# Every matmul of the delta stage set to 128 rows and 128 columns, with zero weights in what is added

## The chip, the cores and the metric

The kernel runs on one core of one Trainium2 chip. The metric is the device time of one execution in microseconds (us), and the median of the runs counts.

## The reference, cut to what matters

A state-space block over an image of 48 x 48 places and 256 channels (two images, four channel groups: 8 units `u`) is followed by attention and a mixture-of-experts layer. The change is in the step that prepares the scan of the first layer, the delta stage:

```python
x = x @ in_W                                   # 64 -> 128 channels
x = conv_general_dilated(x, conv_W, ...)       # 3x3, depthwise
x = silu(x + conv_b)
xs = stack([x0, x1, x0 reversed, x1 reversed]) # 4 directions k
dbl = einsum('bkdl,kcd->bkcl', xs, x_proj_W)
dts, Bmat, Cmat = split(dbl, [4, 20], axis=2)
delta = softplus(einsum('bkrl,kdr->bkdl', dts, dt_W) + dt_b)
... scan over l with delta, delta*u, Bmat, Cmat ...
```

## The kernel before, in words

The program runs in stages, each a block of five instruction streams (TensorE, VectorE, ScalarE, GpSimd, SyncE) that meet through semaphores: setup, norm0, delta, scan, merge, norm1, projection, attention, gate, experts. A stage starts when the one before it has ended.

The delta stage (`delta_phase`, L282 on) has these matmuls, all with 128 output columns but one:

- **convolve** (L412): input projection and 3 x 3 convolution in one. An image tile `img` holds the image twice, in rows 0 to 63 and, shifted by one line, in rows 64 to 127. A block of 384 places (`TT`) takes six taps: three with `w_pair` (128 rows, two image lines at a time) alternate with three with `w_one` (64 rows, the third line; it reads only rows 0 to 63 of `img`). A tap has 384 columns of moving data, or 376 at the image's edges. Each tap is float32, and the profile shows it as two weight loads and two matmuls.
- **project** (L428): 384 places of `xs` or its transposed copy `xt` by `w_bc`, 128 rows by 96 columns, float32, again two loads and two matmuls.
- **expand** (L438, L439): pieces of 512 (`PIECE`) by `w_dt` (104 rows) and then by `w_dt_lo` (64 rows), both float32r, one load and one matmul each. The tile `cut` that they read holds in rows 0 to 39 the projected values as float32r, ones in the rest up to row 63, and in rows 64 to 103 what the rounding left (`lo`).

The work is cut into 16 groups `g` (8 units, 2 pairs of directions `p`), nine pieces each. The order on TensorE is written out by hand: first, ahead of the groups, nine blocks of convolve (six of unit 0, three of unit 1), then six projects for group 0; then for each piece `i` of a group an expand, in six of the nine pieces a project for the next group, and in six pieces three taps of a convolve for a unit to come (so three blocks per group, up to group 12; groups 13 to 15 have none, group 15 has no project either). PSUM holds three pieces of `ps_a`, three of `ps_e`, but one `ps_b` and one `ps_c`: a project waits until ScalarE and VectorE have taken the block before, a convolve until VectorE has copied the block out (L511).

ScalarE makes the magnitude (L475), the exponential (L495), copies of the projected blocks (L470, L471), at the end of a group three logarithms of 1536 (L480) and, in every second group, a silu of the next unit (L461); a table load stands between each kind. VectorE has per piece L547, L551, L555, then the addition of the logarithm for the group before (L525, six per group), and takes the blocks (L511, L517, L519). GpSimd multiplies (L575) and transposes (L567); SyncE stores.

The first thing VectorE does in the stage is to clear `img` and write the ones of `cut` (L528 to L533); the semaphore `cleared` then lets SyncE load the first image, which the first convolve waits for. The weights are made in `setup_phase` (L74 on): `w_one` at L172, `w_dt` at L159, `w_dt_lo` at L181.

Of the kernel before, what the change touches and what calls it, by code (L numbers as in the profile page):

```python
# [6 lines left out]
F32 = mybir.dt.float32  # L7
BF16 = mybir.dt.bfloat16
F32R = mybir.dt.float32r
U32 = mybir.dt.uint32  # L10
I32 = mybir.dt.int32
ALU = mybir.AluOpType
# [8 lines left out]
DM = C // BR  # L21
D = 128
K = 4
R, N = 4, 16
# [2 lines left out]
HW_ = WC // 2  # L27
STEPS = K * NCH
PAIRS = 2
STACK = 104  # L30
PIECE = 512
SOFT = (4, 12)
WARM = (1, 3, 6, 8, 10, 13, 15)
# [3 lines left out]
TT = 384  # L37
# [36 lines left out]
def setup_phase(nc, P, w, keep):  # L74

    with ExitStack() as ctx:
        s = Space(nc, ctx, "setup")
        dt_raw = s.sb("dt_raw", [STACK, K, D])
        x_rows = s.sb("x_rows", [R + 2 * N, K, D])
        conv_taps = s.sb("conv_taps", [128, D, 9])  # L80
        in_w2 = s.sb("in_w2", [128, D])
# [5 lines left out]
        loaded, ones_set, ident_set = s.sem("loaded"), s.sem("ones_set"), s.sem("ident_set")  # L87
# [73 lines left out]
        @block.vector  # L161
        def _(dve):
            dve.wait_ge(exp_done, 1)
            dve.wait_ge(pool_set, 4)
            dve.wait_ge(pool_set, 5)
            dve.tensor_scalar(keep["a_neg"][:, :, :], a_exp[:, :, :], -1.0, None, ALU.mult).then_inc(a_done, 1)

            for dx in range(3):
                for half in range(2):
                    p = slice(64 * half, 64 * half + 64)  # L170
                    dve.tensor_tensor(keep["w_pair"][p, dx, :], in_w2[p, :], conv_taps[p, :, 3 * half + dx], ALU.mult)
                dve.tensor_tensor(keep["w_one"][:, dx, :], in_w2[0:64, :], conv_taps[0:64, :, 6 + dx], ALU.mult)  # L172
            dve.tensor_reduce(keep["d_sum"][:, :], ds4[:, :], AX.X, ALU.add)
            dve.wait_ge(bc_ps, 1)
            for p in range(PAIRS):
                for k in range(2):
                    d = p + 2 * k
                    for to, at, n in ((N * k, R, N), (2 * N + R * k, 0, R), (4 * N + N * k, R + N, N)):
                        dve.tensor_copy(keep["w_bc"][:, p, to:to + n], ps_w[:, d, at:at + n])
            dve.wait_ge(dt_cut, 1)  # L180
            dve.tensor_tensor(keep["w_dt_lo"][:, :, :], dt_raw[0:64, :, :], keep["w_dt"][0:64, :, :].bitcast(F32), ALU.subtract)  # L181


def norm_phase(nc, tag, src, dst, keep):
# [96 lines left out]
def delta_phase(nc, P, keep):  # L281
# [4 lines left out]
    with ExitStack() as ctx:  # L286
# [4 lines left out]
        bc = [s.sb(f"bc{i}", [6 * N, L]) for i in range(2)]  # L291
        cut = [s.sb(f"cut{i}", [STACK, L], F32R) for i in range(2)]
        mag = [s.sb(f"mag{i}", [128, PIECE]) for i in range(3)]
        de = [s.sb(f"de{i}", [128, 2 * L]) for i in range(2)]
        du = [s.sb(f"du{i}", [128, 2 * L]) for i in range(2)]
        ps_a = [s.ps(f"ps_a{i}", [128, PIECE]) for i in range(3)]
        ps_e = [s.ps(f"ps_e{i}", [128, PIECE]) for i in range(3)]
        ps_b = s.ps("ps_b", [128, PIECE])
        ps_c = s.ps("ps_c", [128, PIECE])
        cleared, ones_set, xs_ready, xt_ready = s.sem("cleared"), s.sem("ones_set"), s.sem("xs_ready"), s.sem("xt_ready")  # L300
# [4 lines left out]
        a_full, b_full, c_full, c_taken = (s.sem(x) for x in ("a_full", "b_full", "c_full", "c_taken"))  # L305
        even_taken, odd_taken, hi_done, lo_done = (s.sem(x) for x in ("even_taken", "odd_taken", "hi_done", "lo_done"))
# [85 lines left out]
        @block.tensor  # L392
        def _(pe):
            def convolve(unit, t, first, last):
                o = ps_c[:, 0:TT]
                ov = o.rearrange("p (r w) -> p r w", w=W)
                iv = img[unit % 2][:, :].rearrange("p (r w) -> p r w", w=W)
                r0 = t * (TT // W)
                RB = TT // W
                if first == 0:  # L400
                    if t == 0:
                        pe.wait_ge(img_here[unit % 2], 32 * (unit // 2) + 32)
                    pe.wait_ge(c_taken, unit * TPI + t)
                taps = [(dx, one) for dx in (1, 0, 2) for one in range(2)]
                for n in range(first, last):
                    dx, one = taps[n]
                    a, b = max(0, 1 - dx), min(W, W + 1 - dx)
                    if one:
                        lhs, rows, x = keep["w_one"][:, dx, :], slice(r0 + 2, r0 + 2 + RB), iv[0:64]
                    else:  # L410
                        lhs, rows, x = keep["w_pair"][:, dx, :], slice(r0, r0 + RB), iv
                    mm = pe.matmul(ov[:, :, a:b], lhs, x[:, rows, a + dx - 1:b + dx - 1], start=n == 0, stop=n == 5)  # L412
                if last == 6:
                    mm.then_inc(c_full, 1)

            def project(g, b):
                u, p = divmod(g, PAIRS)
                m = TPI * g + b
                if b == 0:
                    if p == 0:  # L420
                        pe.wait_ge(xs_ready, u + 1)
                    else:
                        pe.wait_ge(xt_ready, u + 1)
                if m:
                    pe.wait_ge(lo_done, m)
                    pe.wait_ge(even_taken, (m + 1) // 2)
                x = xs[u % 3] if p == 0 else xt[u % 2]
                pe.matmul(ps_b[0:6 * N, 0:TT], keep["w_bc"][:, p, :], x[:, b * TT:b * TT + TT], start=True, stop=True).then_inc(b_full, 1)  # L428

            def expand(g, i):  # L430
                n = g * IG + i
                pe.wait_ge(hi_done, TPI * g + blocks_for(i))
                pe.wait_ge(lo_done, TPI * g + blocks_for(i))
                if n >= 3:
                    pe.wait_ge(v_done, n - 2)
                for r, at, a, b in spans(i):
                    d = g % PAIRS + 2 * r
                    pe.matmul(ps_a[n % 3][:, a:b], keep["w_dt"][:, d, :], cut[g % 2][:, at:at + b - a], start=True, stop=False)  # L438
                    mm = pe.matmul(ps_a[n % 3][:, a:b], keep["w_dt_lo"][:, d, :], cut[g % 2][0:64, at:at + b - a], start=False, stop=True)  # L439
                mm.then_inc(a_full, 1)  # L440

            for t in range(TPI):
                convolve(0, t, 0, 6)
            for t in range(3):
                convolve(1, t, 0, 6)
            pe.wait_ge(ones_set, 2)
            for b in range(TPI):
                project(0, b)
            for g in range(G):
                for i in range(IG):  # L450
                    expand(g, i)
                    if proj_block(g, i):
                        project(*proj_block(g, i))
                    if conv_block(g, i) and i % 3 < 2:
                        convolve(*conv_block(g, i), 3 * (i % 3), 3 * (i % 3) + 3)
# [48 lines left out]
        def _(dve):  # L504
# [8 lines left out]
            def take_block(g, b):  # L513
                m = TPI * g + b
                dve.wait_ge(hi_done, m + 1)
                if m % 2:
                    dve.tensor_copy(bc[g % 2][:, b * TT:b * TT + TT], ps_b[0:6 * N, 0:TT]).then_inc(odd_taken, 1)  # L517
                at = slice(b * TT, b * TT + TT)
                dve.tensor_tensor(cut[g % 2][64:STACK, at], ps_b[0:40, 0:TT], cut[g % 2][0:40, at].bitcast(F32), ALU.subtract).then_inc(lo_done, 1)  # L519

            def add_log(g, j):
                at = slice(j * WC, j * WC + WC)
# [4 lines left out]
            for k in range(2):  # L527
                dve.memset(img[k][:, :], 0.0)  # L528
            for k in range(2):
                last = dve.memset(cut[k][32:64, :].bitcast(F32), 1.0)  # L530
                last.then_inc(ones_set, 1)
            last = dve.memset(mag[0][:, 0:1], 0.0)
            last.then_inc(cleared, 1)  # L533
            for t in range(TPI):
# [5 lines left out]
            for g in range(G):  # L540
                for i in range(IG):
                    n = g * IG + i
                    at = slice(i * PIECE, i * PIECE + PIECE)
# [1316 lines left out]
def conv_attn_hybrid_kernel(nc, x, w0, w1, out):  # L1860
# [15 lines left out]
    with ExitStack() as ctx:  # L1876
# [4 lines left out]
        }  # L1881
        scan_shapes = {
            "ones_d": [128, 128], "a_neg": [D, K, N],
            "w_bc": [128, PAIRS, 6 * N], "w_pair": [128, 3, D], "w_one": [DM, 3, D],
            "conv_b": [D, 1], "onorm_g": [D, 1], "onorm_b": [D, 1], "out_W": [D, DM], "d_sum": [D, 1],
            "skip": [DM, 1],
        }
        keep = {name: s.sb(name, shape) for name, shape in shapes.items()}
        with nc.cleanup_on_exit(), ExitStack() as mamba:
            m = Space(nc, mamba, "layer0")  # L1890
            keep |= {name: m.sb(name, shape) for name, shape in scan_shapes.items()}
            keep["b_sel"] = m.sb("b_sel", [128, N, 128], F32R)
            keep["w_dt"] = m.sb("w_dt", [STACK, K, D], F32R)
            keep["w_dt_lo"] = m.sb("w_dt_lo", [64, K, D], F32R)
            setup_phase(nc, P, w0, keep)
            norm_phase(nc, "norm0", x.rearrange("b c y x -> b c (y x)"), P["xn"], keep)
            delta_phase(nc, P, keep)
            scan_phase(nc, P, keep)
            merge_phase(nc, P, keep)
# [37 lines left out]
```

## Time and profile before

| | |
|---|---|
| median of three runs | 6650.8 us (6642.84 to 6655.27) |
| the profiled execution | 6642.5 us, its span 6640.5 us |
| TensorE matmuls, share of the span | 84% |
| VectorE, ScalarE, GpSimd | 67%, 57%, 61% |
| granted TensorE clock, mean over the span | 0.874 of full |

The granted clock has two levels, 0.5 (1.2 GHz) and 1.0 (2.4 GHz). In a view by windows, each row gives the window, its length, and for each engine the busy time and the number of instructions, then the granted clock, the mean busy share of the DMA engines and their rate. In a view by groups of instructions, a row gives line, engine, operation, tiles, shapes, count, busy time, mean ns of one, and the idle time of the engine just before them. For a matmul, `104*128` is rows by columns of the weights. In a timeline, a row gives start, length, and what ran; equal neighbours are merged (x2), and the bracket is idle time of the engine before it with what ended it.

### The profile page before, as it was taken

Reading aid. Unit: us, or ns where it says so; the run is one execution under the profiler, and the core shown is the slowest. Engines: PE = TensorE matmul, PEld = TensorE weight load, DVE = VectorE, ACT = ScalarE, POOL = GpSimd, SP = SyncE. Lnnn points to the kernel's source line nnn. Section 1 sums busy time; section 2 is a strip of 40 time slices with the busy share of each in tenths; the row PEclk is TensorE's granted clock in tenths of the full one; section 3 lists DMA queues with packets and bytes.
Section 4 is the critical chain, followed back from the end, with each engine's and each line's share of the span. In section 5 each row is a group of like instructions: output and inputs, shape, how many; then the busy total and the mean of one; then the engine's idle time right before and its main releaser. Section 6 shows DMA issues by size and latency. Waiting matters only on the chain. (4 is left out here: it accounts for less than half of the span.)

```text
span 6640.5 us, 85890 instructions
## 1 busy us (share of the span) xinstructions
PE 5592.6 (84%) x22476; PEld 3598.1 (54%) x22476; DVE 4455.1 (67%) x4543; ACT 3776.0 (57%) x8015; POOL 4033.4 (61%) x2715
## 2 busy tenths in 40 slices
PE   4888876999989899898998999955579999965995
PEld 2233323555555555555555555532359999944773
DVE  2355568999999999999999999967331111144332
ACT  2234356888778778787877878844542222232232
POOL 0022226999999999999999999953014444412441
PEclk7555557999999999999999999987789999975897
DMA  2133336777777777777777777766200000012213
GB/s 78 67 121 135 121 134 230 247 248 248 245 243 245 238 245 248 239 245 243 246 247 244 245 243 249 249 211 215 91 29 0 0 0 0 0 50 87 76 58 107
DMA packets 399683, 1073.52 MB, mean 162 GB/s; under 512 B 51470, under 2 KB 94511, under 8 KB 393600
## 3 DMA queue, kind: packets, MB, share of 16 engines
q1 hardware_dynamic: 387808, 1043.07, 47.7%
q0 software_dynamic: 7584, 20.72, 1.0%
q10 hardware_dynamic: 3840, 4.72, 0.3%
q8 instruction: 160, 2.62, 0.2%
q14 instruction: 291, 2.38, 0.1%
HBM read 883.39 MB, written 184.94 MB: 161 GB/s over the span
## 5 line engine op out<-in xcount | busy, mean ns | idle before, releaser
L910 POOL TENSOR_TENSOR scan_hc<-scan_h,scan_c_rep 128x768 f32<-128x768 f32 x1536 | 2743.8, 1828 | 257.3 <-PE scan_ps_y L741 224.9
L741 PE MATMUL scan_ps_y<-scan_hc,keep_ident 128*128 128x512 f32 (+1 forms) x6144 | 2223.0, 489 | 24.7 <-ACT scan_y L776 21.1
L875 DVE TENSOR_TENSOR_SCAN scan_h<-scan_da,scan_h,scan_ps_p 128x768 f32<-128x768 f32 x896 | 1573.5, 1795 | 0.0
L741 PEld LDWEIGHTS scan_ps_y<-scan_hc,keep_ident 128*128 128x128 f32 x6144 | 1068.8, 191 | 829.4 <-issue 745.7
L832 ACT ACTIVATE scan_da<-scan_dd,layer_a_neg 128x768 f32<-128x768 f32 x1344 | 1209.7, 926 | 189.0 <-DVE scan_h L875 184.1
L793 ACT ACTIVATE scan_warm<-scan_du_t 128x128 f32<-128x128 f32 x4032 | 1243.4, 389 | 3.8 <-PE scan_ps_p L732 3.2
L1252 POOL TENSOR_TENSOR attn_e_lo<-attn_e,attn_e_hi 128x384 fp32r<-128x384 f32 x432 | 437.1, 1012 | 773.5 <-DVE attn_e_hi L1243 773.5
L875 DVE TENSOR_TENSOR_SCAN scan_h<-scan_da,scan_ps_p 128x768 f32<-128x768 f32 x448 | 760.9, 1734 | 2.0 <-ACT scan_da L832 2.0
L854 DVE TENSOR_TENSOR scan_ps_p<-scan_ps_p,scan_dd 128x768 f32<-128x768 f32 x672 | 634.9, 945 | 134.5 <-PE scan_ps_p L724 132.7
L1243 DVE CAST attn_e_hi<-attn_e 128x384 fp32r<-128x384 f32 x432 | 165.4, 383 | 713.3 <-ACT attn_e L1231 713.3
L732 PE MATMUL scan_ps_p<-keep_ident,scan_warm 128*128 128x128 f32 x4032 | 579.9, 280 | 68.6 <-DVE scan_h L875 63.6
L1231 ACT ACTIVATE attn_e<-attn_ps_s 128x384 f32<-128x384 f32 x432 | 212.6, 492 | 692.6 <-PE attn_ps_s L71 692.6
L724 PE MATMUL scan_ps_p<-scan_cut,layer_b_sel 128*128 128x512 f32 x1344 | 434.4, 404 | 159.0 <-DVE scan_h L875 156.9
L732 PEld LDWEIGHTS scan_ps_p<-keep_ident,scan_warm 128*128 128x128 f32 x4032 | 444.7, 142 | 212.3 <-issue 134.7
L724 PEld LDWEIGHTS scan_ps_p<-scan_cut,layer_b_sel 128*128 128x128 f32 x1344 | 219.2, 190 | 341.1 <-DVE scan_h L875 312.5
L904 POOL TENSOR_TENSOR scan_bu<-scan_dd,scan_b_rep 128x768 f32<-128x768 f32 x192 | 350.5, 1826 | 0.0
L575 POOL TENSOR_TENSOR delta_du<-delta_de,delta_xs 128x768 f32<-128x768 f32 x48 | 86.8, 1808 | 415.4 <-DVE delta_de L525 415.4
L475 ACT ACTIVATE delta_mag<-delta_ps_a 128x512 f32<-128x512 f32 x144 | 85.7, 595 | 433.7 <-PE delta_ps_a L439 433.6
L412 PE MATMUL delta_ps_c<-delta_img,layer_w_pair 128*128 128x376 f32 (+1 forms) x288 | 232.3, 910 | 108.0 <-DVE delta_xs L511 75.3
L547 DVE TENSOR_SCALAR delta_du<-delta_ps_e 128x512 f32<-128x512 f32 x144 | 99.0, 688 | 322.9 <-ACT delta_ps_e L495 322.9
L69 PE MATMUL attn_ps_s<-f_hi,f_lo 128*128 x864 | 293.1, 339 | 2.1 <-DVE attn_t_lo L1239 2.1
L69 PE MATMUL attn_ps_o<-attn_e_hi,attn_t_lo 128*128 128x384 f32 x864 | 291.5, 337 | 3.7 <-POOL attn_e_lo L1252 3.7
(282 smaller groups left out, 8190.4 us busy)
## 6 DMA issues: line engine op xcount, KB each, us to landing
scan_c_rep<-bc_dram SPq DMA_DIRECT2D x1536, 384.0 KB, 4.3
scan_dd<-dd_dram SPq DMA_DIRECT2D x96, 768.0 KB, 5.7
scan_b_rep<-bc_dram SPq DMA_DIRECT2D x192, 384.0 KB, 4.9
dd_dram<-delta_de SPq DMA_DIRECT2D x96, 384.0 KB, 2.4
dd_dram<-delta_du SPq DMA_DIRECT2D x96, 384.0 KB, 3.0
y_dram<-scan_y SPq DMA_DIRECT2D x96, 384.0 KB, 4.6
merge_y<-y_dram SPq DMA_DIRECT2D x32, 1152.0 KB, 10.6
delta_img<-xn_dram SPq DMA_DIRECT2D x16, 576.0 KB, 9.8
```

The costliest lines, as they stand in the source:

```text
L69: pe.matmul(out, wl, xh, start=start, stop=False)
L412: mm = pe.matmul(ov[:, :, a:b], lhs, x[:, rows, a + dx - 1:b + dx - 1], start=n == 0, stop=n == 5)
L724: mm = pe.matmul(ps_p[place(t) % PR][:, lo:hi], keep["b_sel"][:, n, :], cut[st % 2][:, lo:hi], start=True, stop=True)
L732: mm = pe.transpose(ps_p[place(t) % PR][:, b * 128:b * 128 + 128], warm[w % WR][:, b, :], keep["ident"][:, :])
L741: mm = pe.matmul(ps_y[:, lo:hi], keep["ident"][:, :], hc[t % HR][:, lo:hi], start=n == 0, stop=n == N - 1)
L793: last = act.activation(warm[w % WR][:, b, :], du_t[st % 2][:, b * 128:b * 128 + 128], ACT.Identity, scale=du_t[st % 2][:, at:at + 1])
L832: act.activation(dst, dd[st % 2][:, 0, :], ACT.Exp, scale=keep["a_neg"][:, k, n:n + 1]).then_inc(ex_done, 1)
L854: dve.tensor_tensor(x, x, dd[st % 2][:, 1, :], ALU.mult).then_inc(mult_done, 1)
L875: dve.tensor_tensor_scan(view(h[n]), view(x), view(y), start, ALU.mult, ALU.add).then_inc(scan_done, 1)
L904: pool.tensor_tensor(bu[f % SR][:, :], dd[st % 2][:, 1, :], b_rep[f % SR][:, :], ALU.mult).then_inc(bu_done, 1)
L910: pool.tensor_tensor(hc[t % HR][:, :], h[t % N][:, :], c_rep[t % CR][:, :], ALU.mult).then_inc(hc_done, 1)
L1252: pool.tensor_tensor(e_lo[j % 4][:, :], e[j % 4][:, :], e_hi[j % 4][:, :].bitcast(F32), ALU.subtract).then_inc(lo_done, 1)
```

## The change

`STACK` goes from 104 to 128, so `w_dt` and `cut` get 128 rows; `w_dt_lo` and `w_one` get 128 rows with zeros in rows 64 to 127; `w_bc` gets 128 columns with zeros in the last 32. The matmuls with `w_one` now read all 128 rows of `img`, those with `w_dt_lo` all 128 of `cut`. VectorE clears the new parts.

```diff
-STACK = 104
+STACK = 128
...
             dve.wait_ge(pool_set, 4)
+            dve.memset(keep["w_one"][64:128, :, :], 0.0)
+            dve.memset(keep["w_dt_lo"][64:128, :, :].bitcast(F32), 0.0)
...
-                dve.tensor_tensor(keep["w_one"][:, dx, :], in_w2[0:64, :], conv_taps[0:64, :, 6 + dx], ALU.mult)
+                dve.tensor_tensor(keep["w_one"][0:64, dx, :], in_w2[0:64, :], conv_taps[0:64, :, 6 + dx], ALU.mult)
...
-            dve.tensor_tensor(keep["w_dt_lo"][:, :, :], dt_raw[0:64, :, :], keep["w_dt"][0:64, :, :].bitcast(F32), ALU.subtract)
+            dve.tensor_tensor(keep["w_dt_lo"][0:64, :, :], dt_raw[0:64, :, :], keep["w_dt"][0:64, :, :].bitcast(F32), ALU.subtract)
...
                     if one:
-                        lhs, rows, x = keep["w_one"][:, dx, :], slice(r0 + 2, r0 + 2 + RB), iv[0:64]
+                        lhs, rows = keep["w_one"][:, dx, :], slice(r0 + 2, r0 + 2 + RB)
                     else:
-                        lhs, rows, x = keep["w_pair"][:, dx, :], slice(r0, r0 + RB), iv
-                    mm = pe.matmul(ov[:, :, a:b], lhs, x[:, rows, a + dx - 1:b + dx - 1], start=n == 0, stop=n == 5)
+                        lhs, rows = keep["w_pair"][:, dx, :], slice(r0, r0 + RB)
+                    mm = pe.matmul(ov[:, :, a:b], lhs, iv[:, rows, a + dx - 1:b + dx - 1], start=n == 0, stop=n == 5)
...
-                pe.matmul(ps_b[0:6 * N, 0:TT], keep["w_bc"][:, p, :], x[:, b * TT:b * TT + TT], start=True, stop=True).then_inc(b_full, 1)
+                pe.matmul(ps_b[:, 0:TT], keep["w_bc"][:, p, :], x[:, b * TT:b * TT + TT], start=True, stop=True).then_inc(b_full, 1)
...
-                    mm = pe.matmul(ps_a[n % 3][:, a:b], keep["w_dt_lo"][:, d, :], cut[g % 2][0:64, at:at + b - a], start=False, stop=True)
+                    mm = pe.matmul(ps_a[n % 3][:, a:b], keep["w_dt_lo"][:, d, :], cut[g % 2][:, at:at + b - a], start=False, stop=True)
...
-                dve.tensor_tensor(cut[g % 2][64:STACK, at], ps_b[0:40, 0:TT], cut[g % 2][0:40, at].bitcast(F32), ALU.subtract).then_inc(lo_done, 1)
+                dve.tensor_tensor(cut[g % 2][64:104, at], ps_b[0:40, 0:TT], cut[g % 2][0:40, at].bitcast(F32), ALU.subtract).then_inc(lo_done, 1)
...
             for k in range(2):
-                last = dve.memset(cut[k][32:64, :].bitcast(F32), 1.0)
-                last.then_inc(ones_set, 1)
+                dve.memset(cut[k][64:STACK, :].bitcast(F32), 0.0)
+                dve.memset(cut[k][32:64, :].bitcast(F32), 1.0).then_inc(ones_set, 1)
+            dve.wait_ge(ones_set, 2)
             last = dve.memset(mag[0][:, 0:1], 0.0)
             last.then_inc(cleared, 1)
...
-            "w_bc": [128, PAIRS, 6 * N], "w_pair": [128, 3, D], "w_one": [DM, 3, D],
+            "w_bc": [128, PAIRS, 128], "w_pair": [128, 3, D], "w_one": [128, 3, D],
...
-            keep["w_dt_lo"] = m.sb("w_dt_lo", [64, K, D], F32R)
+            keep["w_dt_lo"] = m.sb("w_dt_lo", [STACK, K, D], F32R)
```

## Rows read from the trace of the kernel before

**Rows 1.** Windows over the delta stage, cut where its parts begin.
```profile
115.40:205.40 90.00, 84.69 (x108) 26.96 (x108) 4.46 (x8) 2.21 (x1) 4.07 (x1) 0.50 0.14 36
205.40:232.70 27.30, 19.15 (x27) 6.00 (x26) 5.53 (x10) 7.12 (x14) 0.00 (x0) 0.50 0.03 12
232.70:279.50 46.80, 41.36 (x58) 14.86 (x58) 22.65 (x37) 13.96 (x27) 0.00 (x0) 0.50 0.05 19
279.50:939.80 660.30, 578.43 (x816) 204.29 (x814) 354.85 (x539) 267.83 (x397) 154.97 (x78) 0.52 0.34 126
939.80:1011.20 71.40, 44.95 (x65) 16.32 (x65) 56.76 (x87) 44.37 (x67) 25.87 (x13) 0.50 0.47 179
```

**Rows 2.** Waits of the stage: who for whom, us in total, times, longest.
```profile
ACT delta_mag L475 <- PE delta_ps_a L439: 433.6, 129, 8.0
DVE delta_du L547 <- ACT delta_ps_e L495: 322.9, 81, 8.3
```

**Rows 3.** Timeline of TensorE: taps of the first and second block.
```profile
116.99 1.65 PE L412 MATMUL delta_ps_c<-delta_img,layer_w_one 64*128 64x384 f32 x2
118.56 1.62 PE L412 MATMUL delta_ps_c<-delta_img,layer_w_pair 128*128 128x376 f32 x2
120.11 1.62 PE L412 MATMUL delta_ps_c<-delta_img,layer_w_one 64*128 64x376 f32 x2
...
125.48 1.65 PE L412 MATMUL delta_ps_c<-delta_img,layer_w_pair 128*128 128x384 f32 x2 [0.65 <-DVE delta_xs L511]
```

**Rows 4.** Timeline of weight loads in the norm stage, 384 columns each.
```profile
66.24 0.33 PEld L230 LDWEIGHTS norm_ps_m<-norm_x,keep_ones_c 128*128 128x128 f32 x1 [0.30 <-issue]
66.88 0.33 PEld L230 LDWEIGHTS norm_ps_m<-norm_x,keep_ones_c 128*128 128x128 f32 x1 [0.31 <-issue]
```

**Rows 5.** Windows: the norm stage's second burst, then the early scan stage.
```profile
65.40:68.60 3.20, 3.16 (x5) 1.83 (x6) 0.20 (x1) 0.00 (x0) 0.00 (x0) 0.50 1.02 347
68.60:82.00 13.40, 13.40 (x43) 7.85 (x42) 5.53 (x6) 8.95 (x12) 0.00 (x0) 1.00 0.12 44
...
1162.00:1330.00 168.00, 152.92 (x655) 93.52 (x656) 163.36 (x115) 136.99 (x300) 157.92 (x90) 1.00 0.75 248
```

**Rows 6.** TensorE in a short stretch at full clock: timeline, then window.
```profile
567.81 0.90 PE L412 MATMUL delta_ps_c<-delta_img,layer_w_pair 128*128 128x376 f32 x2
568.64 0.90 PE L412 MATMUL delta_ps_c<-delta_img,layer_w_one 64*128 64x376 f32 x2
...
567.00:573.80 6.80, 4.95 (x13) 1.85 (x12) 4.81 (x8) 4.42 (x9) 0.00 (x0) 1.00 0.13 54
```

**Rows 7.** Logarithms of ScalarE that end groups 12, 13 and 14.
```profile
939.79 4.23 ACT L480 ACTIVATE delta_du<-delta_du 128x1536 f32<-128x1536 f32 x3
...
977.24 1.49 ACT L480 ACTIVATE delta_du<-delta_du 128x1536 f32<-128x1536 f32 x1
...
1011.15 1.48 ACT L480 ACTIVATE delta_du<-delta_du 128x1536 f32<-128x1536 f32 x1
```

**Rows 8.** VectorE by line, in group 14, then in group 1.
```profile
L547 DVE TENSOR_SCALAR delta_du<-delta_ps_e 128x512 f32<-128x512 f32 x10 | 6.8, 684 | 4.8 <-ACT delta_ps_e L495 4.8
...
L511 DVE COPY delta_xs<-delta_ps_c 128x384 f32<-128x384 f32 x3 | 1.6, 548 | 0.0
```

**Rows 9.** The longest wait of VectorE between groups 12 and 13.
```profile
DVE delta_du L547 <- ACT delta_ps_e L495: 7.4, 1, 7.4
```

**Rows 10.** Timeline of VectorE at the start of the stage, and in setup.
```profile
100.50 2.06 DVE L528 MEMSET delta_img<- 128x2400 f32 x1 [0.45 <-issue]
...
105.48 1.98 DVE L530 MEMSET delta_cut<- 32x2304 f32 x1 [0.43 <-issue]
...
25.89 0.68 DVE L181 TENSOR_TENSOR layer_w_dt_lo<-setup_dt_raw,layer_w_dt 64x512 fp32r<-64x512 f32 x1 [10.53 <-ACT layer_w_dt L159]
```

**Rows 11.** Weight loads of the stage by line and shape.
```profile
L412 PEld LDWEIGHTS delta_ps_c<-delta_img,layer_w_pair 128*128 128x128 f32 x288 | 71.4, 308 | 237.2 <-issue 116.9 <-DVE delta_xs L511 87.0 <-DMA delta_img<-xn_dram 33.3
L428 PEld LDWEIGHTS delta_ps_b<-delta_xs,layer_w_bc 128*96 128x96 f32 x96 | 18.7, 255 | 54.8 <-ACT delta_xs L461 23.8 <-DVE delta_cut L519 17.6 <-issue 13.4
```

## Prediction

> **What bounds the kernel now.** I read the windows first, to find the stage. From 115.4 to 1011.2 us TensorE runs nearly all the time at a granted clock of 0.5, that is 1.2 GHz, and it is busy for 84.69 of 90.00 us in the convolve prologue and for 578.43 of 660.30 us in groups 1 to 12 [rows 1]. VectorE is busy only 354.85 us there. The waits say the same: ScalarE waits 433.6 us for `ps_a`, VectorE 322.9 us for the exponential behind it [rows 2]. So in the groups with a convolve TensorE sets the pace.
>
> Groups 13 and 14 have no convolve, and there the bound changes. Their logarithms start 37.45 and 33.91 us after the one before [rows 7], against 660.3 / 12 = 55.0 us in groups 1 to 12. In group 14 VectorE waits once, 4.8 us, for the logarithms and the table load of ScalarE [rows 8]; in group 13, which follows a silu, 7.4 us [rows 9]. The rest it is busy, so these two are VectorE's own pace.
>
> **What a matmul of another width costs today.** Two things show.
>
> First, gaps. A tap of 384 columns takes 118.56 - 116.99 = 1.57 us, one of 376 takes 1.55 [rows 3]. The norm stage has the same float32 matmul with 128 rows each time: its loads stand 66.88 - 66.24 = 0.64 us apart, 1.28 for two, at the same clock [rows 4, 5]. So a tap loses 0.29 to 0.30 us where rows go from 128 to 64 or back. At full clock a tap takes 568.64 - 567.81 = 0.83 [rows 6] against 1.28 / 2 x 376 / 384 = 0.63, a loss of 0.20. By piece kind (expand, three taps; expand, project, three taps; expand, project) the row count crosses 64 four, six and two times, if 104 counts as full; that is 12 in three pieces, 36 in a group.
>
> Second, the clock. The norm burst rose to 1.0 about 3.2 us after its start, all its matmuls having 128 rows [rows 5]. The convolve prologue, 94% busy with 128 and 64 rows in turn, stays at 0.50 for 90 us [rows 1]. That points to rows as what counts. Whether zero weights count is shown by the scan stage: most of its matmuls use the identity as weights, 127 of 128 entries zero, at a clock of 1.00 [rows 5].
>
> The Trainium skill (TensorE: Matmul & The Clock Gate, Part 1) says that the clock follows how busy TensorE has been and names no rows. By that the prologue should have been granted full clock, which the trace contradicts; what the rule would leave of the change is the second rival below.
>
> **The change part by part.**
>
> Setup: two clears on VectorE of 384 and 512 elements, each below the 0.68 us of the same-size subtraction at L181. VectorE waits 10.5 us ahead of L181 [rows 10] for the `dt` loads, which hides them; uncovered they would cost 1.4. Taken at nothing.
>
> Start of the stage: two more clears of 2304 elements ahead of `cleared`. The one with 32 rows takes 1.98 us after a gap of 0.43 [rows 10]; with 64 rows the trace has none. A clear of 2400 elements on 128 rows takes 2.06, so rows don't lengthen it, and I take 2.41 each; were it to go by rows, double. +4.9 us, all on the path, since the first image load and the first tap wait for it. At most +9.6.
>
> Convolve prologue, 90.0 us now: nine blocks, each six taps, and nine waits of 0.65 for VectorE's copy [rows 3]. With no gaps and at full clock a block is 6 x 0.63 = 3.8 us; the first, partly at half clock, 5.5. Together 5.5 + 8 x 3.8 + 9 x 0.65 = 41.8: -48.2. The silu of unit 0 (2.21 us in the prologue window [rows 1]) still ends before the last of these blocks.
>
> Project prologue, 27.3 us [rows 1]: a chain of TensorE, ScalarE and VectorE for each of six blocks; TensorE idles in every link of it, so I count no clock and only the shorter matmul, about 0.2 each: -1. With full clock -5.
>
> Group 0, 46.8 us [rows 1], of which VectorE is busy 22.65. With a wait like group 14's 4.8 and some 5 us for taps at half clock just after the idle stretch: about 33, -14.
>
> Groups 1 to 12, 660.3 us. TensorE: busy 578.43 / 12 = 48.2 us a group; without 36 gaps of 0.295, 37.6; at full clock 18.8. VectorE: group 14's pace plus three copies of `ps_c`, 1.6 us and their starts [rows 8], so 33.9 + 1.7 = 35.6, and 37.45 + 1.7 = 39.1 after a silu. TensorE at 18.8 lies well below, so VectorE is late next: 6 x 35.6 + 6 x 39.1 = 448. But during VectorE's wait TensorE runs out of buffers, idles and may lose the clock, as it did after 573.8, where it had been busy 4.95 of 6.80 us [rows 6], and the next taps restart at half rate. It is two to three pieces ahead, which covers most of this; I leave 1 us a group. 448 + 12 = 460: -200. Bounds: ScalarE further ahead could hide one or two logarithms, 1.4 us a group less; the upper bound is rival one.
>
> Groups 13 to 15 and the tail are at VectorE's pace already: nothing. GpSimd was busy 25.87 and DMA 0.47 of 71.4 us at that pace [rows 1], so neither takes over. The 32 more columns of `w_bc` lengthen its load from 255 to about 308 ns [rows 11], hidden behind the matmul before once widths are equal, as in the norm stage.
>
> Sum: 4.9 - 48.2 - 1 - 14 - 200 = -258. Against the profiled execution's 6642.5 us that is 6384; the median of the runs stands 8.3 above it, so **6392 us**. This case alone: 6365 to 6420.
>
> **The rivals.**
>
> *One, the clock is lost in every group and costs more.* For: VectorE's pace keeps TensorE busy only half the time, and one short idle took the clock at 573.8. Against: TensorE even at half clock needs 37.6 us a group, about what VectorE needs. If each group loses 3 to 5 us instead of 1, +24 to +48: 6416 to 6440.
>
> *Two, the clock doesn't follow rows and only the gaps go.* Then the prologue loses 54 x 0.295 = 16, groups 1 to 12 lose 12 x 36 x 0.295 = 127, group 0 10, project 1, plus 4.9: -149, 6502. Against: the norm and the prologue differ in rows above all. For: another cause, such as how the taps' rows are read, can't be excluded. This is also the time where zero rows aren't counted for the clock. It is what the Trainium skill's rule (TensorE: Matmul & The Clock Gate, Part 1) would come to, if equal widths remove the gaps.
>
> *Three, neither follows width*: gaps belong to changing weights, the clock to something else. Against: the identity and other weights alternate in the scan stage at full clock. Then only the clears are left, 6656, no change that can be measured.
>
> *Four, slower.* As three, with the gaps before each load kept and the `w_bc` load exposed: 192 loads of 53 ns more, 10.2 us [rows 11], with the clears 15: 6666. It decides from 13.3 us on, which is 0.2%, about what a measurement of this kernel can tell from no change.
>
> **How the numbers follow.** Forecast 0.73, rival one 0.12, two 0.08, three 0.05, four 0.02. Faster by over 0.2%: the first three, 0.93; within 0.2% 0.05; slower 0.02. The range starts below the forecast's own, since logarithms hidden behind VectorE would take 17 more and two executions differ by 10: 6355. It ends at 6450, with rival one inside; rivals two to four and a small part of the forecast, under 0.2 together, are left out.
>
> **What would show it.** Right: clock near 1.0 from about 125 us until the first project, a tap at 0.64 us; 4.9 us from the last old clear to the new start; groups 35 to 41 us apart, with VectorE waiting 3 to 8 us once a group; groups 13 to 15 unchanged. Wrong: clock at 0.5 through the prologue with taps at 1.28 (rival two) or 1.57 (three); inside the groups many waits of VectorE for the exponential (rival one); time gained or lost behind the delta stage.

## The result, and the profile after

The changed kernel runs in 6383.4 us (median of four, 6381.9 to 6389.1) against 6647.2 for the kernel before (four runs, the three shown and one more): ratio 0.960, 95% interval 0.959 to 0.962. Faster by 264 us, 4.0%. The forecast was 6392, with 6365 to 6420 for this case alone and 6355 to 6450 as the whole range.

The windows over the delta stage, cut at the same events as in [rows 1] (first tap, first project, logarithms of groups 0, 12 and 14):

```profile
121.90:167.00 45.10, 38.96 (x110) 20.93 (x110) 5.01 (x9) 2.96 (x3) 4.10 (x1) 0.96 0.28 71
...
214.80:676.50 461.70, 323.49 (x816) 178.59 (x816) 348.74 (x540) 261.45 (x398) 155.61 (x78) 0.83 0.49 180
676.50:746.80 70.30, 38.02 (x64) 16.23 (x64) 56.60 (x86) 44.31 (x66) 25.92 (x13) 0.51 0.48 184
```

The same number of matmuls (816) in groups 1 to 12 takes 461.7 us instead of 660.3, and the granted clock is 0.83 instead of 0.52. VectorE's busy time is unchanged (348.7 against 354.9 us), but it is now 76% of the stretch instead of 54%. Groups 13 and 14 take 70.3 us, as before within 1.1. (The first window here runs 1.7 us past the first project, which starts at 165.4: the prologue itself is 43.4 us.)

The waits of groups 1 to 12 (engine and line, who was waited for, us in total, times, longest), two of the kernel before and then three of the changed one; [rows 2] count the whole stage. VectorE waits far less for the exponential, three times a group instead of six. TensorE waits for VectorE's copy of `ps_c` as often as before, but longer:

```profile
DVE delta_du L547 <- ACT delta_ps_e L495: 276.4, 72, 8.3
PE delta_ps_c L412 <- DVE delta_xs L511: 66.4, 36, 2.7
...
DVE delta_du L550 <- ACT delta_ps_e L497: 102.8, 36, 7.7
PE delta_ps_c L414 <- DVE delta_xs L513: 99.5, 36, 3.0
PE delta_ps_b L430 <- ACT delta_xs L463: 18.8, 6, 3.3
```

The timeline of the first taps answers to [rows 3] and [rows 4]:

```profile
121.91 1.65 PE L414 MATMUL delta_ps_c<-delta_img,layer_w_pair 128*128 128x384 f32 x2 [37.63 <-DMA delta_img<-xn_dram]
123.35 1.48 PE L414 MATMUL delta_ps_c<-delta_img,layer_w_one 128*128 128x384 f32 x2
124.63 1.05 PE L414 MATMUL delta_ps_c<-delta_img,layer_w_pair 128*128 128x376 f32 x2
125.52 0.80 PE L414 MATMUL delta_ps_c<-delta_img,layer_w_one 128*128 128x376 f32 x2
126.15 0.80 PE L414 MATMUL delta_ps_c<-delta_img,layer_w_pair 128*128 128x376 f32 x2
```

The second tap (`w_one`, now 128 rows) starts 1.28 us before the third at half clock, where it took 1.57 before. From 125.1 us on the clock is full, and a tap takes 0.63 us. From there on each tap of the prologue is therefore 2.5 times as fast as it was.

Where the 258 us between the two profiled executions (6642.5 and 6384.8) are:

| part | before, us | after, us | difference |
|---|---|---|---|
| up to the first tap | 115.4 | 121.9 | +6.5 |
| convolve prologue | 90.0 | 43.4 | -46.6 |
| first project to the logarithms of group 0 | 74.1 | 49.5 | -24.6 |
| groups 1 to 12 | 660.3 | 461.7 | -198.6 |
| groups 13 to 15 | 98.5 | 97.2 | -1.3 |
| all that follows | 5604.2 | 5611.1 | +6.9 |

The last row runs from the last logarithms of the delta stage to the end. Of its 6.9 us, 2.6 lie between these logarithms and the scan stage's first instruction (23.8 us before, 26.4 after). From that instruction to the end of the span it is 5578.4 and 5582.8 us; the instructions there are the same, and over the twelve profiles of this study that part varies from 5578 to 5598 us. So I don't lay those 4.4 us to the change, but no run shows that it has no share in them.

### The profile page after: what moved, and what is told of

It is laid out like the page before. It is cut to its first block and busy times, and to the rows that moved or that the text cites. A ratio compares the mean times of both kernels' runs of the same rounds, so it can differ in the third digit from the quotient of the medians.

```text
span 6382.9 us, 85894 instructions
## 1 busy us (share of the span) xinstructions
PE 5254.0 (82%) x22476; PEld 3561.1 (56%) x22476; DVE 4453.9 (70%) x4547; ACT 3769.1 (59%) x8015; POOL 4035.1 (63%) x2715
## 5 line engine op out<-in xcount | busy, mean ns | idle before, releaser
L71 PE MATMUL attn_ps_s<-f_hi 128*128 x864 | 293.8, 340 | 0.0
L70 PE MATMUL attn_ps_s<-f_lo,f_hi 128*128 x864 | 292.6, 339 | 0.0
L71 PE MATMUL attn_ps_o<-attn_e_hi,attn_t_hi 128*128 128x384 f32 x864 | 291.6, 337 | 0.0
L70 PE MATMUL attn_ps_o<-attn_e_lo,attn_t_hi 128*128 128x384 f32 x864 | 290.2, 336 | 0.0
```

Source lines behind the costliest of these rows:

```text
L70: pe.matmul(out, wh, xl, start=False, stop=False)
L71: return pe.matmul(out, wh, xh, start=False, stop=stop)
```

## The experiments

Two causes were in play, which the kernel before mixes: **gaps** where the row count crosses 64, and the **clock**. Of the clock I had claimed that it follows active rows; the rival is that it was kept low by the gaps themselves, since matmuls without gaps are also denser. "Prologue" below is first tap to first project.

### Half of the change at a time

`e1_conv_only` is the kernel before with only the third-line taps widened:

```diff
+            dve.memset(keep["w_one"][64:128, :, :], 0.0)
...
-                        lhs, rows, x = keep["w_one"][:, dx, :], slice(r0 + 2, r0 + 2 + RB), iv[0:64]
+                        lhs, rows, x = keep["w_one"][:, dx, :], slice(r0 + 2, r0 + 2 + RB), iv
```

> Only the convolve's third-line taps (w_one) get 128 rows; expand and project stay as before. Theory (rows carry the clock, each crossing of 64 rows costs a gap of 0.2 to 0.3 us, VectorE's pace is the floor): the convolve prologue is like that of the changed kernel, about 45 us at clock 1.0; in the groups 18 crossings are left instead of 36, TensorE needs about 43 us a group at half clock and 22 at full, so VectorE still sets nearly all of the pace: 6385 to 6410 us. Rival (the 104- and 64-row matmuls hold the clock at 0.5 inside the groups): 48 us a group, about 6490.

`e2_expand_only` is the changed kernel with those taps narrow again:

```diff
-                        lhs, rows = keep["w_one"][:, dx, :], slice(r0 + 2, r0 + 2 + RB)
+                        lhs, rows, x = keep["w_one"][0:64, dx, :], slice(r0 + 2, r0 + 2 + RB), iv[0:64]
```

> Everything widened but the convolve, whose third-line taps keep 64 rows. Theory: the convolve prologue stays at clock 0.5 with taps of 1.55 us, 90 us, 45 more than in the changed kernel; in the groups 18 crossings and mostly half clock, 46 to 50 us a group: 6500 to 6550 us. Rival (it is the expand's rows that hold the clock down in the groups, and the convolve's matter little there): groups near 38.5 us as in the changed kernel, 6430.

Measured: 6411.4 us, ratio 0.963 (0.961 to 0.965), and 6510.0 us, ratio 0.978 (0.976 to 0.979). Their windows, prologue and groups 1 to 12, the first kernel first:

```profile
116.80:160.90 44.10, 38.80 (x108) 21.05 (x109) 4.46 (x8) 2.22 (x1) 4.10 (x1) 0.95 0.29 74
217.30:702.50 485.20, 373.93 (x816) 180.13 (x816) 350.03 (x541) 263.26 (x397) 155.32 (x78) 0.77 0.47 171
```

```profile
123.30:213.30 90.00, 84.70 (x109) 26.96 (x109) 4.46 (x8) 2.22 (x1) 4.07 (x1) 0.50 0.14 36
270.90:803.50 532.60, 405.13 (x816) 175.22 (x816) 352.30 (x541) 261.29 (x397) 155.25 (x78) 0.74 0.42 156
```

The convolve carries most: with it alone the prologue is won and the groups fall to 40.4 us each; 248 of 264 us are there, and the total is 1 us above the range that theory gave it. The other half alone leaves the prologue at 90.0 us and half clock, to the tenth of a microsecond the old one. In its groups I was off: I expected mostly half clock and 46 us or more, and got 0.74 and 44.4. A group's mix of wide taps, expands and projects lifts the clock although every third-line tap stays narrow. So neither half needs the other, and their gains don't add.

### Gaps or rows

`e5_gap_full` gives the changed kernel its gaps back without taking a row away; the small matmul adds zero:

```diff
+                    if n:
+                        pe.matmul(ov[:, 0, 0:8], keep["w_one"][64:128, 0, :], img[unit % 2][64:128, 0:8], start=False, stop=False)
                     mm = pe.matmul(ov[:, :, a:b], lhs, iv[:, rows, a + dx - 1:b + dx - 1], start=n == 0, stop=n == 5)
```

> The changed kernel, with a tiny matmul of 64 rows and 8 columns with zero weights between the taps of the convolve, so that each tap has its gaps back while its rows stay 128. Theory (rows count for the clock): clock 1.0 in the prologue, a tap about 0.9 to 1.0 us, prologue 55 to 60 us. Rival (what kept the clock low before was the gaps, not the rows): clock 0.5 in the prologue, a tap about 1.7 us, prologue 95 to 100 us.

`e9_conv_80` does the opposite. All taps use 80 rows, so nothing crosses 64, and a part of the contraction is left out:

```diff
-                        lhs, rows = keep["w_one"][:, dx, :], slice(r0 + 2, r0 + 2 + RB)
+                        lhs, rows, x = keep["w_one"][0:80, dx, :], slice(r0 + 2, r0 + 2 + RB), iv[0:80]
...
-                        lhs, rows = keep["w_pair"][:, dx, :], slice(r0, r0 + RB)
+                        lhs, rows, x = keep["w_pair"][0:80, dx, :], slice(r0, r0 + RB), iv[0:80]
```

> The changed kernel, but all taps of the convolve use only the first 80 rows (a part of the contraction is left out). No tap crosses 64 rows, so no gaps. Theory (active rows carry the clock): clock 0.5 in the prologue, taps of 1.28 us without gaps, prologue about 75 us. Rival (gaps kept the clock low): clock 1.0, taps 0.64 us, prologue 45 us. If 80 rows had gaps against 128, taps would show 1.55 us.

The prologue of the kernel with gaps in two windows, then two taps of its timeline at full clock, with the small matmul between them:

```profile
121.40:138.00 16.60, 15.95 (x30) 7.22 (x30) 0.56 (x1) 0.00 (x0) 0.00 (x0) 0.51 0.22 47
138.00:193.40 55.40, 50.75 (x171) 25.11 (x171) 3.90 (x7) 2.21 (x1) 4.10 (x1) 1.00 0.16 43
...
151.50 0.91 PE L416 MATMUL delta_ps_c<-delta_img,layer_w_one 128*128 128x384 f32 x2
152.34 0.39 PE L415 MATMUL delta_ps_c<-delta_img,layer_w_one 64*128 64x8 f32 x2
152.66 0.90 PE L416 MATMUL delta_ps_c<-delta_img,layer_w_pair 128*128 128x376 f32 x2
```

And the prologue of the kernel with 80 rows, then its timeline:

```profile
119.80:196.30 76.50, 71.21 (x109) 35.16 (x110) 4.46 (x8) 2.21 (x1) 4.08 (x1) 0.50 0.17 42
...
122.50 1.46 PE L414 MATMUL delta_ps_c<-delta_img,layer_w_pair 80*128 80x376 f32 x2
123.75 1.46 PE L414 MATMUL delta_ps_c<-delta_img,layer_w_one 80*128 80x376 f32 x2
125.00 1.46 PE L414 MATMUL delta_ps_c<-delta_img,layer_w_pair 80*128 80x376 f32 x2
```

This tells the two apart. With wide rows and gaps the clock is full for the last 55 of 72 us. With 80 rows and no gaps (taps 1.25 us apart, which is the 1.28 of 384 columns scaled to 376) it never leaves 0.50, though TensorE is busy for 71.21 of 76.50 us. So gaps alone don't hold the clock down, and narrow rows alone do. Gaps are not without effect on it, though: the rise came 16 us after the first tap. I had the size wrong in the first kernel: I had taken no such delay, and a tap with its small matmul takes 1.16 us at full clock (151.50 to 152.66), not 0.9 to 1.0; so the prologue was 72.0 us, not 55 to 60. With its groups at 573.9 us the total is 6536.7, one run.

The second kernel also shows the gap alone, apart from the clock: 76.5 us of prologue against 90.0 is the 13.5 us that gaps cost there. I had counted 54 gaps, 16 us, in rival two; but the gap behind a block's last tap falls in with the wait for VectorE's copy, and the 45 inside the blocks come to 45 x 0.30 = 13.5. Of the 46.6 us that the prologue lost, the other 33.1 are the clock's. Its total, 6462.5 us, is one run.

The Trainium skill (TensorEngine Tiling (Array Packing), Tiling Modes) says under Key Properties that changing the tiling mode drains TensorE, and lists 64 rows under another mode than 128. Where the gaps stand agrees with that: there are 0.30 us a tap between 128 and 64 rows [rows 3] and none between 128 and 96, as the next kernels' taps show.

### How wide is wide enough, and do columns count

`e3_one_96` gives the third-line taps 96 rows in the changed kernel, `e8_bc_96` the project its old 96 columns:

```diff
-                        lhs, rows = keep["w_one"][:, dx, :], slice(r0 + 2, r0 + 2 + RB)
+                        lhs, rows, x = keep["w_one"][0:96, dx, :], slice(r0 + 2, r0 + 2 + RB), iv[0:96]
```

```diff
-                pe.matmul(ps_b[:, 0:TT], keep["w_bc"][:, p, :], x[:, b * TT:b * TT + TT], start=True, stop=True).then_inc(b_full, 1)
+                pe.matmul(ps_b[0:6 * N, 0:TT], keep["w_bc"][:, p, 0:6 * N], x[:, b * TT:b * TT + TT], start=True, stop=True).then_inc(b_full, 1)
```

> The changed kernel with the third-line taps at 96 rows instead of 128, the result the same. Theory (rows above 64 make no gap; the clock goes by active rows, which are 112 on average here): prologue 43 to 46 us at clock near 1.0, total 6380 to 6400 us. Rival (any change of the row count makes a gap): taps 0.20 us longer at full clock, prologue about 54 us, groups 3 to 4 us longer, 6440 us.

> The changed kernel with the project matmul at 96 columns as before, its output again 96 partitions. Theory (rows alone count, columns neither for gaps nor for the clock): as the changed kernel, within 0.2%, 6378 to 6392 us. Rival (columns count too): project matmuls get gaps of 0.2 us and the clock falls oftener, groups 1 to 2 us longer, 6395 to 6410.

Measured: 6390.0 us (one run) and 6386.5 us, ratio 0.960 (0.958 to 0.962). With 96 rows, two taps of the timeline at full clock (0.63 us apart, as with 128) and the window of the groups; then that window with 96 columns:

```profile
132.25 0.80 PE L414 MATMUL delta_ps_c<-delta_img,layer_w_one 96*128 96x376 f32 x2
132.88 0.80 PE L414 MATMUL delta_ps_c<-delta_img,layer_w_pair 128*128 128x376 f32 x2
...
220.50:681.50 461.00, 327.00 (x816) 179.73 (x816) 349.04 (x541) 261.60 (x396) 155.61 (x78) 0.82 0.49 180
```

```profile
215.30:678.40 463.10, 324.28 (x816) 175.21 (x816) 348.68 (x540) 261.64 (x397) 155.69 (x78) 0.82 0.49 180
```

Both are the changed kernel within what can be told. The 32 added columns do nothing here, and rows up to 96 do all that 128 do, where the other taps have 128.

### The same taps in another order

`e6_grouped` adds no row to the kernel before; the six taps only stand as three wide and three narrow:

```diff
-                taps = [(dx, one) for dx in (1, 0, 2) for one in range(2)]
+                taps = [(dx, one) for one in range(2) for dx in (1, 0, 2)]
```

> The kernel before with its six taps in another order: the three with 128 rows first, then the three with 64; no row is added. Theory: 24 crossings a group instead of 36, a block of the prologue has 2 instead of 6, and taps of equal width stand 1.26 to 1.28 us apart at half clock whether 64 or 128 rows; prologue about 80 us at clock 0.5, or less if three wide taps in a row lift the clock; groups about 50 us; 6530 to 6590 us. Rival (64 rows are slow in themselves): no change, 6645 to 6655.

Measured: 6457.6 us (one run), far below the expected 6530. Prologue and groups, then a stretch of the timeline at full clock:

```profile
116.80:164.60 47.80, 42.50 (x109) 20.55 (x109) 4.46 (x8) 2.21 (x1) 4.09 (x1) 0.91 0.27 67
221.70:754.00 532.30, 434.01 (x816) 192.92 (x816) 353.08 (x541) 264.11 (x397) 155.19 (x78) 0.67 0.43 156
...
131.16 2.17 PE L412 MATMUL delta_ps_c<-delta_img,layer_w_one 64*128 64x384 f32 x6
133.98 2.17 PE L412 MATMUL delta_ps_c<-delta_img,layer_w_pair 128*128 128x384 f32 x6 [0.65 <-DVE delta_xs L511]
```

Six records, three taps, take 2.17 us whether they have 64 or 128 rows. So 64 rows are not slow in themselves; the crossing is. And with three wide taps in a row the clock was 0.91 in a prologue with exactly the rows, on average, that stayed at 0.50 in turn. I had put the block order down as a question of gaps and mentioned the clock as a possibility; it was most of the effect: in the prologue four of five gaps in each block are gone, 9 x 4 x 0.30 = 10.8 us, and it lost 42.2. So the average of rows over the taps does not decide the clock by itself. Whether the three in a row lift it or the missing gaps do was not taken apart, since this edit changes both. One changed line, with nothing padded, gives 2.9%.

### A shorter start

The added clears stand ahead of the first image load, where VectorE then idles 13.4 us for the first block. `e7_short_start` clears the margins of the image tiles alone before `cleared`, and does the rest of `cut` after it:

```diff
             for k in range(2):
-                dve.memset(img[k][:, :], 0.0)
+                dve.memset(img[k][0:64, 0:W], 0.0)
+                dve.memset(img[k][0:64, W + L:L + 2 * W], 0.0)
+                last = dve.memset(img[k][64:128, L:L + 2 * W], 0.0)
+            last.then_inc(cleared, 1)
             for k in range(2):
                 dve.memset(cut[k][64:STACK, :].bitcast(F32), 0.0)
                 dve.memset(cut[k][32:64, :].bitcast(F32), 1.0).then_inc(ones_set, 1)
             dve.wait_ge(ones_set, 2)
-            last = dve.memset(mag[0][:, 0:1], 0.0)
-            last.then_inc(cleared, 1)
```

> The changed kernel with a shorter start of the stage: VectorE clears only the margins of the image tiles before it lets the first image load go, and clears and fills the rest of cut after that, while it would wait for the first convolve. Theory: about 14 us of clears leave the path (4.6 to 5 for the image, 10 for cut), 6368 to 6374 us. Rival (the image load, which would now start earlier, is held by something else, such as the stores of the stage before): no gain, 6383.

Measured: 6373.2 us (6369.2 to 6374.4, five runs), ratio 0.958 (0.956 to 0.959): the fastest kernel of this study, 10 us below the changed one, whose four runs all lie above these five. Its timeline at the start of the stage:

```profile
99.96 0.14 DVE L532 MEMSET delta_img<- 64x96 f32 x1
100.12 0.53 SPq L347 DMA_DIRECT2D delta_img<-xn_dram  x1
100.53 1.98 DVE L535 MEMSET delta_cut<- 64x2304 f32 x1 [0.43 <-issue]
...
108.02 1.65 PE L414 MATMUL delta_ps_c<-delta_img,layer_w_pair 128*128 128x384 f32 x2 [23.43 <-DMA delta_img<-xn_dram]
```

The load goes at 100.1 and the first tap at 108.0 instead of 121.9, with the clears behind the load. That is 13.9 us of the 14 expected; the profiled executions differ by 14.1 us, the medians by 10.2.

### Is VectorE's wait for the logarithms the next bound?

`e10_mag_after` moves one magnitude behind the first exponential of a group; `e11_logs_later` adds to it that the logarithms of a group are made after the second exponential of the next, and added one piece later. Both contain the short start.

```diff
-                    if n + 1 < G * IG:
+                    if n + 1 < G * IG and i:
                         magnitude(n + 1)
...
+                    if i == 0:
+                        magnitude(n + 1)
```

```diff
+                    if i == 1 and g:
+                        for r in range(LOGS):
+                            log(g - 1, r)
-                for r in range(LOGS):
-                    log(g, r)
...
+            for r in range(LOGS):
+                log(G - 1, r)
...
-                    if g and 0 < i <= CG:
-                        add_log(g - 1, i - 1)
+                    if g and 1 < i <= CG + 1:
+                        add_log(g - 1, i - 2)
```

> The kernel with the short start, and in the first piece of a group ScalarE makes the exponential before the magnitude of the next piece, instead of after it. Theory (VectorE's one wait per group, behind logarithms, table load, magnitude and exponential, sets the pace): 0.6 us off each of 15 waits, 9 us: 6362 to 6366 us against 6373. Rival (TensorE at half clock sets the pace, the wait of VectorE only shows it): under 3 us of change.

> As the kernel before it in this list, and ScalarE makes a group's three logarithms after the second exponential of the next group instead of ahead of the first; VectorE adds them one piece later. VectorE then has two pieces in hand while ScalarE changes tables. Theory (VectorE's wait is the bound): 2 to 4 us off a group, 30 to 60 us: 6305 to 6340 us. Rival one (TensorE is next, at 30 us busy in a group at mixed clock): a gain of 5 to 15 us only, 6350 to 6360. Rival two (stores of a group end one piece later and hold VectorE at the start of the next but one): no gain or a loss.

Measured: 6376.2 us (6370.2 to 6383.2), not told from the kernel with the short start alone; and 6440.3 us (6420.7 to 6443.7), 67 us slower than that kernel. In the profile of the first, groups 1 to 12 took 456.2 us instead of 463.2, close to what was expected of them, but the stages from the scan on took 8.4 us more, and the medians show no gain. VectorE's waits for the exponential fell there from 104.4 to 84.0 us, and 8.4 us of waits for the stores, which the other kernel does not have, came in. So it is inconclusive. The second is a plain miss. Its waits and clock over 200 us of its groups:

```profile
DVE delta_du L556 <- ACT delta_ps_e L497: 39.1, 14, 4.8
DVE delta_du L556 <- DMA dd_dram<-delta_du: 18.4, 4, 6.0
...
300.00:500.00 200.00, 141.83 (x322) 77.26 (x320) 139.93 (x215) 102.72 (x157) 63.92 (x33) 0.74 0.47 171
```

VectorE now also waits for the stores of the group before the last (rival two), and the wait for the exponential, 14 times in under five groups, is still there. The clock is 0.74; it was 0.82 in the groups of the kernel with the short start alone. With the stage this close to balance, a wait that is taken from one place came back in two others. Which share the lower clock has in the 67 us is not shown.

## Why the prediction was right

**The bound.** That VectorE's own pace would be late next, at 35.6 and 39.1 us a group, held: groups 1 to 12 took 461.7 us where the sum had 460, and their 36 waits of VectorE for the exponential, 102.8 us, are 8.6 us a group against the 4.8 and 7.4 taken. They came three to a group, where the prediction had one. The even total hides errors that cancel: single groups are further apart than said, from 34.6 to 42.5 us. From the third group on the same four lengths repeat, 42.5, 34.6, 38.8 and 37.8 us. Three in a row, by windows from logarithm to logarithm:

```profile
292.17:334.70 42.53, 30.01 (x68) 16.85 (x68) 29.20 (x46) 23.48 (x34) 11.38 (x7) 0.76 0.55 194
334.70:369.27 34.57, 23.38 (x68) 12.69 (x68) 29.00 (x46) 20.06 (x33) 14.58 (x7) 0.95 0.44 171
369.27:408.06 38.79, 25.88 (x68) 14.23 (x68) 29.11 (x46) 23.48 (x35) 11.42 (x7) 0.87 0.60 208
```

VectorE is busy 29.0 to 29.2 us in each; nearly all the rest is waiting (12.4, 4.8 and 8.8 us), and it goes with the clock. The first and the third both follow a silu and do the same work, one at 0.76 in 42.5 us, the other at 0.87 in 38.8. The best groups are 1 us better than the floor that I took from group 14. The longest wait of VectorE in them is 3.7 us, not 4.8, which fits a ScalarE further ahead, as the lower bound had it; the worst lose 3.4 us, which is what rival one had asked for, but only in some groups. That the clock is the cause and not only goes along was not tested by itself. TensorE was busy 27 us a group, not 18.8: that figure held for full clock throughout, which wasn't granted.

**The clock** rose 3.2 us after the first tap (125.1 against 121.9), as in the norm stage, and the experiments bear out that rows count for it, zero weights included. They are not all of it: the old kernel's taps in another order, no row added, got 0.91, and gaps put the rise off to 16 us. The rule of the Trainium skill that the clock goes by how busy TensorE is (TensorE: Matmul & The Clock Gate, Part 1) fails here twice: at 94% busy in the old prologue, whose busy time takes in the gaps, and at 93% with 80 rows and no gaps. The changed prologue got 0.96 at 86% busy (its first window above).

**The gaps** were as sized, if not as counted: 1.57 us to 1.28 at half clock, 0.83 to 0.63 at full. How the groups' own gain divides between gaps and clock stays open: the kernel with 80 rows has no gaps in its taps, but its clock rose in the groups too, to 0.72, with 41.3 us a group; the one with gaps has 47.8 us at 0.75, but its small matmuls take time of their own.

**The other terms.** Clears: +5.0 of the 6.5 us at the start, predicted 4.9 (the rest came in ahead of the delta stage); the clear on 64 rows took the 1.98 us of the one on 32. Convolve prologue -46.6, predicted -48.2. From the first project to the end of group 0 -24.6, predicted -15 (-1 and -14): here the sum was mis-sized. I gave group 0 some 5 us of taps at half clock and took no clock for the pieces that begin in the project prologue's window; in the run 0.70 was granted from 167 to 190 us and 0.91 from there to the end of group 0. The 6.9 us that the part behind the delta stage's logarithms took more offset most of it. Against the profiled execution the sum said 6384, and it was 6384.8; that it came this close is luck, since 9.6 us too little taken here met smaller errors of the other sign. Nearly all of the difference between 6392 and the measured 6383.4 is the 8.3 us by which the three runs' median stood above the profiled execution: in the changed kernel the median is 1.4 us below it.

## What to carry to other kernels

Where small and full matmuls alternate on TensorE, look at the row counts before the busy share: the granted clock of a window and the distance of two starts tell within two rows whether clock or gaps are lost. Padding narrow matmuls with zero rows cost nothing per instruction here, and even ordering them so that wide ones stand together raised the clock, to 0.91 in the prologue and 0.67 in the groups. Then ask what is next in line (here VectorE, which capped the gain), and put the clears that the padding needs behind the first load.

## What the runs showed of the hardware that was not expected

- 96 rows beside 128 do as well as 128 beside 128 (6390.0 us, clock 0.93 in the prologue), while 80 rows throughout leave the clock at 0.50 for 76.5 us.
- The project's columns made no difference: 96 or 128, 6386.5 and 6383.4 us.
- The order of the same matmuls decided the clock: 0.50 with wide and narrow taps in turn, 0.91 with three of each in a row.
- In the prologue with gaps the clock rose 16 us after the first tap, in the changed kernel 3.2 us after it. With 96 and 128 rows in turn it took some 6 us.
